# The stores of a normalized node table move from SyncE's queue to ScalarE's

## The reference

```python
edge_index = jnp.stack([src, dst])
x = x + gnn(edge_index, layernorm(x), edge_type, weight, h_bias, loop_weight)
x = x + ffn(layernorm(x)[None], mask, wr, br, w1, b1, w2, b2)[0]

# gnn(edge_index, x, ...), with 8 relations
hx = einsum('ni,rio->rno', x, weight)
agg = segment_sum(hx[edge_type, src], dst, num_segments=6250)
return agg * 0.5 ** 0.5 + h_bias + (x @ loop_weight) * 0.5 ** 0.5

# ffn(x, ...): a router picks half of the nodes
weights = x @ wr + br
sel = indices of the 3124 largest weights
y = (gelu(x[sel] @ w1 + b1) @ w2 + b2) * weights[sel]
return x + (y at the selected nodes, 0 elsewhere)
```

## Time and profile before

| what | value |
|---|---|
| time of the profiled execution | 2,123.41 us |
| its span, first to last instruction | 2,121.7 us |
| TensorE busy | 1,738.5 us, 82% |
| GpSimd busy | 1,521.4 us, 72% |
| VectorE busy | 792.3 us, 37% |
| ScalarE busy | 728.9 us, 34% |
| mean granted TensorE clock | 0.941 of full speed |
| moved by DMA | 265.87 MB, mean 125 GB/s |

### The profile page before, as it was taken

How to read it: one execution, slowest core, us unless ns; L and a number is a source line. 1 busy time by engine, 2 the same in 40 slices (tenths; PEclk the granted TensorE clock), 3 DMA queues, 4 the chain that set the end, 5 groups by cost and what they waited for, 6 DMA issues and landing times.

```text
span 2121.7 us, 30502 instructions
## 1 busy us (share of the span) xinstructions
PE 1738.5 (82%) x8696; PEld 1476.8 (70%) x8696; DVE 792.3 (37%) x1854; ACT 728.9 (34%) x1511; POOL 1521.4 (72%) x1615
## 2 busy tenths in 40 slices
PE   0599888888888789888888888888888888888882
PEld 0478776777777677777767777776776777777772
DVE  6644333333333433433333343333333334333336
ACT  5543423243233333324323333332333333333242
POOL 6477777777777777777777777777777777777730
PEclk9999999999999999999999999999999999999895
DMA  9943433433433433443343443333333343343336
GB/s 305 326 133 107 125 107 108 126 107 107 127 106 108 124 109 106 117 117 106 117 116 107 116 117 106 116 115 107 117 116 107 112 122 105 107 126 106 105 105 197
DMA packets 126309, 265.87 MB, mean 125 GB/s; under 512 B 32206, under 2 KB 72957, under 8 KB 126138
## 3 DMA queue, kind: packets, MB, share of 16 engines
q0 software_dynamic: 76704, 209.56, 34.2%
q1 hardware_dynamic: 37002, 42.02, 6.1%
q10 hardware_dynamic: 12432, 12.32, 1.7%
HBM read 244.53 MB, written 19.25 MB: 124 GB/s over the span
## 4 chain that ended last, share of the span: by engine, by line
POOL 51%; PE 18%; issue 17%; DVE 4%; DMA 4%; ACT 3%; SPq 1%; DVEq 0%; ACTq 0%; POOLq 0%
POOL messages L474 51%; PE bank L779 7%; PE bank L811 4%; DMA messages<-normed_table,gather_rows 3%; PE bank L832 3%; PE bank L842 2%; SPq L366 1%; DVE acc L1272 1%; PE bank L789 1%; ACT hidden L646 1%; ACT L646 1%; ACT messages L566 1%; PE bank L813 1%; DMA acc<-in_src 0%; DMA w_sb<-in_x 0%
## 5 line engine op out<-in xcount | busy, mean ns | idle before, releaser
L474 POOL DMA_INDIRECT messages<-normed_table,gather_rows x1562 | 1484.3, 950 | 501.4 <-issue 464.3
L779 PE MATMUL bank<-messages,onehot 128*128 128x256 f32 x3196 | 849.3, 403 | 257.9 <-DMA messages<-normed_table,gather_rows 249.5
L779 PEld LDWEIGHTS bank<-messages,onehot 128*128 128x128 f32 x3196 | 588.6, 198 | 369.7 <-DMA messages<-normed_table,gather_rows 293.9
L1115 DVE SCALAR_TENSOR_TENSOR sums<-bank,regular,sums 128x256 f32 x538 | 260.0, 483 | 1220.7 <-PE bank L789 1179.0
L600 ACT ACTIVATE stage<-bank 128x256 f32<-128x256 f32 x538 | 207.6, 386 | 1297.1 <-PE bank L779 1274.0
L811 PE MATMUL bank<-rel_sb,closed 128*128 128x256 f32 x1568 | 355.0, 379 | 0.7 <-ACT closed L608 0.6
L811 PEld LDWEIGHTS bank<-rel_sb,closed 128*128 128x128 f32 x1568 | 297.4, 190 | 42.8 <-ACT closed L608 2.0
L1034 DVE TENSOR_TENSOR onehot<-bank,keys 128x768 f32<-128x768 f32 x269 | 254.6, 947 | 0.1
L832 PEld LDWEIGHTS bank<-normed_t,w_sb 128*128 128x128 f32 x1568 | 222.2, 225 | 6.0
L832 PE MATMUL bank<-normed_t,w_sb 128*128 128x128 f32 x1568 | 218.6, 306 | 0.0
L789 PE MATMUL bank<-ident,stage 128*128 128x128 f32 x1076 | 209.5, 277 | 9.2 <-ACT stage L600 8.7
(11 more groups left out here) (163 smaller groups left out, 634.4 us busy)
## 6 DMA issues: line engine op xcount, KB each, us to landing
side<-normed_table SPq DMA_DIRECT2D x2048, 1.0 KB
messages<-normed_table,gather_rows POOLq DMA_INDIRECT x1562
acc<-in_x SPq DMA_DIRECT2D x12, 512.0 KB
residual<-resid ACTq DMA_DIRECT2D x12, 512.0 KB
node_out<-acc SPq DMA_DIRECT2D x12, 512.0 KB
normed_x<-normed_table ACTq DMA_DIRECT2D x11, 512.0 KB
messages<-residual SPq DMA_DIRECT2D x6, 896.0 KB, 11.1
rel_sb<-in_L_gnn_weight SPq DMA_DIRECT2D x2, 1024.0 KB, 7.5
```

The lines of the kernel that those rows point to most:

```text
L474: pool.indirect_dma_start(messages[0:EP, g % RING, j * D:(j + 1) * D], None, x if g < RAW else table, bass.IndirectOffsetOnAxis(ap=gather_ ...
L779: last = nc.tensor.matmul(banks[g % STAGES][:, 0:D], onehot[0:EP, g % SLOTS, j, :], rows, start=(j == 0), stop=(j == J - 1))
L1115: V.scalar_tensor_tensor(sums[:, :, to], banks[TURNS[g % 2]][:, 0:D].rearrange("p (n m) -> p n m", m=W), regular[:, 0:1], sums[:, :, to], ...
```

## The change

Each store is issued by ScalarE, right behind the rows of its chunk, after a wait for those rows. SyncE's seven waits and stores are gone; all else stays.

```diff
             sp.dma_start(side_rows[:, :], src[side_from:side_from + SIDED * side_span].rearrange("(q e) -> q e", e=side_span)[:, side_span - P:side_span]
                          ).then_inc(side_rows_in, 16)
 
-            def store(c):
-
-                sp.wait_ge(norm_ready, c + 1)
-                sp.dma_start(table_chunks[c], chunk_rows[c]).then_inc(stored, 16)
-
-            for c in range(NCH):
-                store(c)
             for to, a in ((bias_b, h_bias), (b2_b, b2)):
...
                 if c + 1 < NCH:
                     deviate_chunk(c + 1)
                 norm_chunk(c)
+                act.wait_ge(norm_ready, c + 1)
+                act.dma_start(table_chunks[c], chunk_rows[c]).then_inc(stored, 16)
             act.wait_ge(src_in, 16 * 3)
```

## The result

The changed kernel takes 2,135.26 us (median of five, 2,133.58 to 2,136.8) against 2,125.38 us for the kernel before in the runs beside it: a ratio of 1.0050, 95% interval 1.0035 to 1.0064, 10 us slower. The forecast was 2,134.2 us. The execution profiled has a span of 2,133.6 us.

A forecast was written before the change was run, and what follows sets the result against it. The prediction took one queue of GpSimd gathers to bound the kernel, after a start ending with TensorE's sums. Its terms, 0 + 0 + 10.8 = 10.8 us on 2,123.41 us, gave 2,134.2 us, range 2,124 to 2,142.

The forecast's parts named there:

- What bounds the kernel, and the rigid shift: GpSimd's gathers: the end follows their unbroken start at a fixed distance; the 16.9 us store wait is off the path.
- Removed from SyncE: SyncE's seven waits and stores, behind the edge loads in its program: taking them away gains 0 us.
- Added to ScalarE: Seven waits and issues on ScalarE, two on the path to the edge-source conversion: 0.74 us, covered by a 1.44 us wait.
- ScalarE's issue is held: Rival: ScalarE's store issues stand while SyncE's is held, conversion 7.5 us later, 2,130.9 us; chance 0.20.
- the upper end: Of the price of a store issue on ScalarE: 1.4 us each, 2.8 us for the two on the path.
- Moved: Stores of chunks 0 to 4, now ahead of the edge sources, take engine time from the loads: 10.8 us, ends 8.3 and 19.2.
- All five stores are through before them: Edge sources, behind chunk 6's load in one queue, land after the stores of chunks 0 to 4: 62.1 instead of 51.3.
- Both of ScalarE's conditions move together: Before ScalarE's conversion: chunk 6 slips from 39.4 to about 50 us, the edge sources from 51.3 to 62.1.
- The idle engines: DMA engines at 30 to 40 us: 2.5 us idle, none of it helping because chunk 6's load sits on four engines.
- Hidden: Rival: store packets yield to the loads or use only idle engines, sources still at 51.3, 2,123.4 to 2,125 us; chance 0.14.
- faster: Rival: stores land early and GpSimd's first stop goes, restarting 10.9 us sooner, 2,112.5 us; chance 0.08.
- far worse: Rival: the moved stores run at 239 GB/s throughout, plus 19.2 us, 2,142.6 us; chance 0.04.

The follow-up runs named there:

- e1: The changed kernel, but ScalarE issues all seven stores together after converting the edge sources: 2,130.23 us, ratio 1.0023 to the kernel before.
- e2: The changed kernel, but the stores of chunks 5 and 6 go back to SyncE behind the edge loads: 2,132.31 us, ratio 1.0037 to the kernel before.
- e8: The kernel e3 with chunk 6's load placed behind chunk 2's instead of chunk 5's: 2,115.46 us, ratio 0.9958 to the kernel before.
- e3: The kernel before with chunk 6's load cut in two, 112 partitions and 12: 2,111.65 us, ratio 0.9940 to the kernel before.
- e4: The changed kernel with chunk 6's load cut in two, 112 partitions and 12: 2,131.11 us, ratio 1.0030 to the kernel before.
- e5: The changed kernel with each store cut in two, packets of 4,096 and 3,072 bytes: 2,141.31 us, ratio 1.0065 to the kernel before.

## Why the prediction was right, and where it was not

**What bounds the kernel, and the rigid shift: right.** The end followed the release. The wait for the stores was off the path: it gave 8 us back and nothing came of it.

**Removed from SyncE, 0 us: right.** Its small loads went out near 51 us as before, the weights 8 us sooner (59.67), and nothing waited for either.

**Added to ScalarE, 0.74 us and covered: right here.** Each issue took 0.34 to 0.39 us, also in the middle of SyncE's hold of 21.14 us, so the rival "ScalarE's issue is held" is refuted by the trace. ScalarE was done 2.9 us later, of which chunk 6's later arrival is 1.9; the 1.0 left is a little over 0.74, and covered by its 10.36 us of waiting. e1 shows issues near the upper end to be real elsewhere.

**Moved, 10.8 us: the amount right, its parts not.** The sources were forecast for 62.1 and came at 62.75; the first one-hot for 85 and came at 85.03; the first sum's release for 89.5 and came at 89.25. Two steps behind these numbers failed, and cancelled:

- "All five stores are through before them", and no others: the last two held up the sources as well (e2). Seven stores are 6.42 MB, 15.1 us at 424 GB/s, where the text had 10.8.
- "Both of ScalarE's conditions move together: chunk 6 from 39.4 to about 50": it came at 41.27, 1.9 us late. I took the loads to lose what the stores gain. But the engines that were full from 20 to 28 us in the kernel before moved only 239 GB/s; with the stores among them they moved 365, and 400 from 31 to 39. So the first five stores went in part into engine time that had moved little before, and cost 7.0 us at the sources (e2), not 10.8. e8 found what chunk 6's load does to its neighbours, in the layout of e3; that the same load makes the 239 GB/s here is likely, and not shown.

So 7.0 + 4.4 = 11.4 us at the sources, against 10.8 in the text: the time came out so near because one error took away what the other added, which is luck. As the loads lost less than the stores moved, SyncE's hold stayed at 21.14 us where I wrote over 25, ScalarE was done at 52.8 and not 61.4, the last store was issued at 52.42 and not at 61.4, and GpSimd's wait for it halved, where I expected it about as long as before; its wait for the first sum was 22 us, not 14. Of the signs that were to show the forecast right, the hold, chunk 6's statistics at 48 to 52 us and the two waits of GpSimd did not come.

**The idle engines: wrong.** The step said that the stores can't use the idle of 30 to 40 us because the late load sits on few engines. The changed kernel's stretches, for the earlier trace rows:

```profile
30.00:35.00 5.00, 0.00 (x0) 0.00 (x0) 0.00 (x0) 3.60 (x8) 3.78 (x4) 1.00 1.03 393
35.00:40.00 5.00, 0.00 (x0) 0.00 (x0) 0.00 (x0) 0.00 (x0) 3.79 (x4) 1.00 1.02 409
```

The shares rose from 0.87 and 0.63 to 1.03 and 1.02, so the engines that stood idle did work now, and the five stores' 7.0 us lie under even the 8.3 that gave them all of the idle. That the load sits on few engines fits e3: cut into 112 and 12 partitions it lands before 26.58 instead of 39.36, as the rule on how many engines a load gets would have it (Trainium skill, "DMA: Bandwidth & Descriptors", "Why a DMA increments its semaphore by 16 and not by 1"). But e4 shows that this does not limit the harm: with that load cut, the stores cost 19.5 us instead of 10. The decisive fact is the order: stores behind the edge loads on one queue, or beside them on two.

**The rivals.** "Hidden", "faster" and "far worse" fall with the conversion at 62.75 and the release at 102.32; the stop for the stores did shrink by 8 us, as "faster" wanted. The Trainium skill's rule that a second issuer only saves issue time (same page, "Issuing engines are not separate DMA queues") is right that the queues interleave on the same engines: in e4 the stores held 59.7% of them beside the loads. That the time therefore stays is not what the runs show. A second queue also takes away an order that one queue had kept.

**Open:** why chunk 6's load slows the others, by its rows of x or its place in SBUF, and why stores beside it lift the rate; and why the added turns of e5 brought chunk 6 only 0.3 us sooner. No run issues the stores as early on SyncE's own queue, so what the second queue does, beyond letting the stores go before the edge loads are through, is not set apart.

## What to carry to other kernels

One queue is also a priority: with the stores behind them on SyncE's queue the edge sources were there by 38.4 us (e3), with the stores on a second queue at 57.0 (e4), because there the bulk transfer passed the small loads, packet by packet. Before freeing a wait, look what stands behind it in time: here 17 us of waiting was worth nothing, and the load that VectorE waited 12.91 us for the earlier trace rows was worth 13 us, with its one issue made into two. Ask of each load how many engines carry it.

## What the runs showed of the hardware that was not expected

- Three queues moved 308, 308 and 310 packets in 8 us, with shares of 59.7, 26.4 and 16.0% (e4); with smaller store packets two of them moved 375 and 374, with 41.1 and 32.4% (e5).
- Full DMA engines are not a full rate: 214 GB/s at a share of 1.00 in e3 (20 to 25 us), 404 at 1.01 ten us earlier.
- The same store cost its issuer 0.34 us as one issue among ScalarE's rows (changed kernel) and 1.29 us as the last of seven in a row (e1).
